# First cross-attention: second scores on 99 rows of the query parts, no rows cleared, first query tile split on VectorE

## The reference, cut to what matters

```python
x = _layernorm(x + _L0_xattn_ref(x, ctx_512, ctx_512), axis=-1)

def _L0_xattn_ref(q, k, v):              # q (4, 512, 512); k = v = ctx_512 (4, 512, 128)
    H, KV, D, G = 32, 8, 16, 4           # 32 query heads on 8 key heads, 16 wide
    qh = q.reshape(B, S, KV, G, D).transpose(0, 2, 3, 1, 4)
    kh = k.reshape(B, S, KV, D).transpose(0, 2, 1, 3)
    vh = v.reshape(B, S, KV, D).transpose(0, 2, 1, 3)
    scores = jnp.einsum('bkgsd,bktd->bkgst', qh, kh) / 4
    weights = jax.nn.softmax(scores, axis=-1)
    out = jnp.einsum('bkgst,bktd->bkgsd', weights, vh)
    return out.transpose(0, 3, 1, 2, 4).reshape(B, S, E)
```

## Time and profile before

| | us |
|---|---|
| median of 3 runs | 5124.7 |
| lowest, highest | 5121.35, 5125.94 |
| the profiled execution's own time | 5129.01 |
| its span, first to last instruction | 5127.8 |
| busy: PE, PEld, DVE, ACT, POOL | 4467.1, 2365.1, 2998.9, 1684.2, 1697.6 |
| mean granted clock of TensorE | 0.931 |

### The profile page before, as it was taken

One profiled execution on the slowest core, in us unless ns is written; L12 is line 12 of the kernel. 1 busy time (PEld: TensorE's weight loads), 2 busy tenths in 40 slices (PEclk: granted clock), 3 DMA queues, 4 the chain that ended last, 5 costly groups with the idle time before them and its releaser, 6 DMA issues.

```text
span 5127.8 us, 65483 instructions
## 1 busy us (share of the span) xinstructions
PE 4467.1 (87%) x22744; PEld 2365.1 (46%) x22744; DVE 2998.9 (58%) x5723; ACT 1684.2 (33%) x3306; POOL 1697.6 (33%) x1861
## 2 busy tenths in 40 slices
PE   7996888899999758887999888849999999798688
PEld 6773222244445543554333333325555555343466
DVE  5885777678876986884555565642332333456622
ACT  1112676622113324664222222212112111355432
POOL 1224222000115863552011112455555554211511
PEclk9997999999998678999999999879999999899899
DMA  4330000010000002000012010118999996400000
GB/s 139 98 93 15 2 2 2 35 55 1 0 0 1 1 10 113 2 1 29 25 29 61 25 45 27 26 29 209 245 233 238 217 224 129 143 1 17 3 15 19
DMA packets 154390, 327.66 MB, mean 64 GB/s; under 512 B 25841, under 2 KB 39665, under 8 KB 152498
## 3 DMA queue, kind: packets, MB, share of 16 engines
q1 hardware_dynamic: 106370, 222.50, 13.4%
q0 software_dynamic: 46976, 100.56, 10.1%
q10 hardware_dynamic: 720, 0.40, 0.0%
HBM read 377.91 MB, written 79.30 MB: 89 GB/s over the span
## 4 chain that ended last, share of the span: by engine, by line
PE 64%; DVE 17%; ACT 6%; POOL 5%; issue 4%; DMA 3%; SPq 0%; DVEq 0%; ACTq 0%; POOLq 0%
PE ps L205 59%; PE ps L210 4%; DVE arena L867 2%; ACT arena L2406 2%; ACT arena L841 1%; DVE ps L1386 1%; DVE ps L1409 1%; DMA moe_y<-arena 1%; DVE arena L2432 1%; POOL moe_slots L2133 1%; DVE arena L248 1%; ACT arena L834 1%; ACT arena L1771 1%; DVE arena L1378 1%; DVE arena L2448 1%
## 5 line engine op out<-in xcount | busy, mean ns | idle before, releaser
L205 PE MATMUL ps<-arena 128*128 128x512 f32 (+14 forms) x18488 | 3918.9, 455 | 369.3 <-ACT arena L1786 50.6
L205 PEld LDWEIGHTS ps<-arena 128*128 128x128 f32 (+3 forms) x18488 | 1842.2, 165 | 2250.2 <-issue 1199.9
L210 PE MATMUL ps<-arena 128*128 128x128 f32 (+2 forms) x3232 | 421.1, 270 | 253.3 <-DVE arena L266 54.7
L210 PEld LDWEIGHTS ps<-arena 128*128 128x128 f32 (+2 forms) x3232 | 344.0, 140 | 425.0 <-issue 200.4
L2891 POOL DMA_INDIRECT moe_y<-arena x191 | 304.9, 1596 | 303.6 <-DVE arena L2860 236.4
L256 POOL TENSOR_SCALAR arena<-arena 128x1 f32<-128x1 f32 x160 | 52.7, 330 | 925.1 <-DVE arena L250 922.4
L2406 ACT ACTIVATE arena<-ps 128x1024 f32<-128x1024 f32 (+3 forms) x256 | 166.2, 701 | 576.2 <-PE ps L205 576.2
L867 DVE TENSOR_REDUCE arena<-ps 128x2 f32<-128x1024 f32 x256 | 303.8, 1218 | 85.9 <-PE ps L205 85.1
L2432 DVE TENSOR_REDUCE arena<-ps 128x2 f32<-128x256 f32 (+3 forms) x256 | 198.8, 819 | 260.4 <-PE ps L205 260.4
L2843 DVE SCALAR_TENSOR_TENSOR arena<-ps,arena 128x128 f32<-128x128 f32 x382 | 103.5, 312 | 411.8 <-ACT arena L2830 409.9
L841 ACT ACTIVATE arena<-ps 128x512 f32<-128x512 f32 x512 | 277.6, 597 | 129.2 <-PE ps L205 126.6
(11 more groups left out here) (312 smaller groups left out, 3939.8 us busy)
## 6 DMA issues: line engine op xcount, KB each, us to landing
arena<-in_L_ffn_gu SPq DMA_DIRECT2D x191, 768.0 KB
arena<-in_L_ffn_dn SPq DMA_DIRECT2D x191, 256.0 KB
arena<-in_L_ffn_dn SPq DMA_DIRECT2D x191, 128.0 KB
arena<-in_L_ffn_w SPq DMA_DIRECT2D x64, 256.0 KB
moe_y<-arena SPq DMA_DIRECT2D x34, 256.0 KB
arena<-in_L_ffn_w_gate SPq DMA_DIRECT2D x32, 256.0 KB
arena<-in_L_ffn_w_up SPq DMA_DIRECT2D x32, 256.0 KB
arena<-in_L_ffn_w_down SPq DMA_DIRECT2D x32, 256.0 KB
```

The source lines that it names most:

```text
L205: return self.nc.tensor.matmul(out, lhsT, rhs, start=start, stop=stop, skip_group_check=True)
L210: return self.nc.tensor.transpose(out, in_, ident[0:n, 0:n])
```

## The change

The second scores contract over 99 rows of `KS` and `QS`. Rows 99 to 127 are read by nothing any more, so `QS` is not cleared, and all of columns 96 to 127 of `kst` are set to ones by one memset, which now stands ahead of the two for `VA`. SyncE's wait for the clears is gone. The nine instructions of the query split become the function `qsplit`, issued on VectorE for tile 0 and on GpSimd for tiles 1 to 15. In `order()`, the split of tile 0 stands ahead of the key tiles. The query transposes of tile 0 wait for VectorE, those of the others for GpSimd, as before.

```diff
--- before.py
+++ after.py
@@ -712,10 +712,10 @@
     qv = qst.rearrange("p h (r d) -> p h r d", d=16)
 
     def order():
+        yield "qsplit", 0, 0
         for t4 in range(4):
             yield "prep", 0, t4
             yield "prep2", 0, t4
-        yield "qsplit", 0, 0
         yield "qt", 0, 0
         yield "qt", 0, 1
         for n in range(16 * NT + LAG + 11):
@@ -755,11 +755,31 @@
     def loads():
         for b in range(4):
             dma.start(sp, CX[:, 4 * b:4 * b + 4, :], ins["ctx_512"][b].rearrange("(t p) d -> p t d", p=P), "ctx", b)
-        sp.wait_ge(pool, "qs0")
         for i in range(NT):
             sp.wait_ge(dve, "mr", i)
             sp.wait_ge(pe, "pv", i - 3, 7) if i >= 3 else None
             dma.start(sp, QS[i % 3][96:99, :, :], MT[i % 2][0:96, :], "mrow", i)
+
+    def qsplit(unit, by, i):
+
+        part = [qv[:, :, r, :] for r in range(6)]
+        sc, res = (a.rearrange("p (h d) -> p h d", d=16) for a in (qsc, qres))
+        by.wait_ge(pool if i > 1 else dve, "qparts", i - 1)
+        unit.tensor_scalar(qsc, k.X[:, i, :], 0.25, 1.0, ALU.mult, ALU.mult).then_inc(*by.done("qsc", i))
+        by.wait_ge(by, "qsc", i)
+        by.wait_ge(pe, "qt", i - 1, 3) if i else None
+        unit.tensor_copy(part[0], sc).then_inc(*by.done("qhi", i))
+        by.wait_ge(by, "qhi", i)
+        unit.tensor_tensor(res, sc, part[0], ALU.subtract).then_inc(*by.done("qr1", i))
+        unit.tensor_copy(part[1], part[0]).then_inc(*by.done())
+        unit.tensor_copy(part[4], part[0]).then_inc(*by.done())
+        by.wait_ge(by, "qr1", i)
+        unit.tensor_copy(part[2], res).then_inc(*by.done("qmid", i))
+        by.wait_ge(by, "qmid", i)
+        unit.tensor_tensor(res, res, part[2], ALU.subtract).then_inc(*by.done("qr2", i))
+        unit.tensor_copy(part[3], part[2]).then_inc(*by.done())
+        by.wait_ge(by, "qr2", i)
+        unit.tensor_copy(part[5], res).then_inc(*by.done("qparts", i))
 
     def tensor():
         for what, i, j in order():
@@ -772,7 +792,7 @@
                 t.then_inc(*pe.done("kt", i, j))
             elif what == "qt":
                 s1 = S1.take("qt", i, j, by=((act, "q", i, 2 * j + 1),))
-                pe.wait_ge(pool, "qparts", i)
+                pe.wait_ge(pool if i else dve, "qparts", i)
                 for u in range(2):
                     bb = s1[:, u, :].bitcast(BF16).rearrange("p (h n) -> p h n", n=P)
                     for h in range(8):
@@ -794,7 +814,7 @@
                 v, t4 = tile(j)
                 bb = S2.take("s2", i, j, by=((act, "p", i, j),))
                 pe.wait_ge(dma, "mrow", i)
-                k.mm(bb, KS[b % 2][:, v, t4 * P:t4 * P + P], QS[i % 3][:, 4 * v:4 * v + 4, :].rearrange("p h n -> p (h n)"), True,
+                k.mm(bb, KS[b % 2][0:99, v, t4 * P:t4 * P + P], QS[i % 3][0:99, 4 * v:4 * v + 4, :].rearrange("p h n -> p (h n)"), True,
                      True).then_inc(*pe.done("s2", i, j))
             elif what == "pv":
                 j, t4 = divmod(j, 4)
@@ -850,7 +870,9 @@
     def vector():
         former = -1, 0
         for what, i, j in order():
-            if what == "prep":
+            if what == "qsplit" and i == 0:
+                qsplit(nc.vector, dve, 0)
+            elif what == "prep":
                 dve.wait_ge(dma, "ctx", i)
                 dve.wait_ge(pool, "kst0")
                 if former[0] >= 0:
@@ -891,15 +913,9 @@
                 k.norm(i)
 
     def gpsimd():
+        nc.gpsimd.memset(kst[:, :, 96:128], 1.0).then_inc(*pool.done("kst0"))
         for buf in VA:
             nc.gpsimd.memset(buf[:, :, :, 16:32], 1.0).then_inc(*pool.done("ones"))
-        nc.gpsimd.memset(kst[:, :, 96:128], 0.0).then_inc(*pool.done("kst00"))
-        pool.wait_ge(pool, "kst00")
-        nc.gpsimd.memset(kst[:, :, 96:99], 1.0).then_inc(*pool.done("kst0"))
-        pool.wait_ge(pool, "kst0")
-        for buf in QS:
-            nc.gpsimd.memset(buf[96:128, :, :], 0.0).then_inc(*pool.done("qs0"))
-        pool.wait_ge(pool, "qs0")
         for what, i, j in order():
             if what == "prep":
                 pool.wait_ge(dma, "ctx", i)
@@ -910,25 +926,8 @@
                 pool.wait_ge(dve, "kparts", i, j)
                 for dst, src in ((2, 0), (3, 1), (5, 0)):
                     nc.gpsimd.tensor_copy(kv[:, :, dst, :], kv[:, :, src, :]).then_inc(*pool.done("kparts", i, j))
-            elif what == "qsplit":
-                part = [qv[:, :, r, :] for r in range(6)]
-                sc, res = (a.rearrange("p (h d) -> p h d", d=16) for a in (qsc, qres))
-                pool.wait_ge(pool, "qparts", i - 1)
-                nc.gpsimd.tensor_scalar(qsc, k.X[:, i, :], 0.25, 1.0, ALU.mult, ALU.mult).then_inc(*pool.done("qsc", i))
-                pool.wait_ge(pool, "qsc", i)
-                pool.wait_ge(pe, "qt", i - 1, 3) if i else None
-                nc.gpsimd.tensor_copy(part[0], sc).then_inc(*pool.done("qhi", i))
-                pool.wait_ge(pool, "qhi", i)
-                nc.gpsimd.tensor_tensor(res, sc, part[0], ALU.subtract).then_inc(*pool.done("qr1", i))
-                nc.gpsimd.tensor_copy(part[1], part[0]).then_inc(*pool.done())
-                nc.gpsimd.tensor_copy(part[4], part[0]).then_inc(*pool.done())
-                pool.wait_ge(pool, "qr1", i)
-                nc.gpsimd.tensor_copy(part[2], res).then_inc(*pool.done("qmid", i))
-                pool.wait_ge(pool, "qmid", i)
-                nc.gpsimd.tensor_tensor(res, res, part[2], ALU.subtract).then_inc(*pool.done("qr2", i))
-                nc.gpsimd.tensor_copy(part[3], part[2]).then_inc(*pool.done())
-                pool.wait_ge(pool, "qr2", i)
-                nc.gpsimd.tensor_copy(part[5], res).then_inc(*pool.done("qparts", i))
+            elif what == "qsplit" and i:
+                qsplit(nc.gpsimd, pool, i)
             elif what == "over":
                 k.norm_rstd(i)
```

## The result

| | before | after |
|---|---|---|
| median of 14 runs each, us | 5125.9 | 5110.5 |
| lowest, highest | 5117.6, 5133.6 | 5102.9, 5115.8 |
| span of the profiled execution | 5127.8 | 5108.9 |
| mean granted clock in it | 0.931 | 0.935 |

The ratio of the runs is 0.9972 with a 95% interval of 0.9964 to 0.9980: 14.4 us faster, between 10.3 and 18.5. The interval of one set is thus 8 to 9 us wide, and the size of the gain is better read from the stage's own length in the trace.

What follows compares the result with a forecast made beforehand. The prediction took the first cross-attention's opening, a chain of single steps, as the bound. Key preparation's 5.5 us plus 5.6 to the first scores made 11.1, taking the median from 5124.7 to 5113.6; range 5108 to 5119.5.

Steps and rivals of the forecast that it cites:

- one of its own signs: First score matmul of the first cross-attention: forecast near 451; wrong if after 453.5 or before 449.5.
- The other two signs: Wrong if the loop to the next stage changes by over 3 us, or 99-row operations differ by over 10 ns.
- The bound: First cross-attention's opening: a chain of single steps, 35.1 us in which TensorE does only 64 small transposes.
- The clears hold VectorE: Stage opening: three GpSimd clears, 10.57 us, hold VectorE's key casts (3.17 for two instead of 0.23 each) and delay GpSimd's copies.
- The split's length: First query split on VectorE, nine instructions: 4.66 us plus 0.8 waiting for memsets, ending at 432.4.
- The first rival: Query split or port lock dearer, split ending up to 434.9: gain 8.6 to 10.2, time 5114.5 to 5116.1; chance 0.22.
- The key preparation: First key split 1.41 us, 0.88 to transposes at 434.7 instead of 440.17; fourth key tile 10.22 later.
- From the last key tile: Fourth key tile at 444.95, then ScalarE's copies are late; first scores at 450.95 instead of 462.04.
- 99 rows: 512 second-score matmuls in the loop: zero cost taken; rival 0.05 us each, 25.6 us, time 5139.2, chance 0.03.
- The clock: TensorE's clock after the first scores: rival has it rise earlier, 4 us more, gain 15, time 5109.6; chance 0.12.
- Within or beyond 0.2%: Whole kernel, resolution 10.25 us (5114.4): faster beyond it 0.62, within it 0.31, slower 0.07.
- the later clock: TensorE's clock rises later or dips once more in the loop: 4 us lost, gain 7, time 5117.7; chance 0.09.

Runs made afterwards that it cites:

- the second: The changed kernel measured again with no edit: ratio 0.9981 to the kernel before, 9.7 us faster, stage of 573.3 us.
- e2: Changed kernel, clears out and 99 rows, but first query split left on GpSimd behind the key tiles: ratio 0.9989 to before, first scores at 27.8 us.
- e3: Changed kernel with GpSimd's clears and 128 rows kept, first query split on VectorE: ratio 0.9991 to before, first scores at 31.9 us.
- e7: Changed kernel with GpSimd's two VA memsets moved behind the key preparation: one run, query split 3.69 us, first scores at 22.16 us.
- e1_rows99: Kernel before with only the second scores cut to 99 rows, clears and GpSimd split kept: ratio 1.0005 to before, loop 551.4 us.

## Why the prediction was right

The forecast was 11.1 us and 5113.6; the opening lost 12.96 and the median of the first set was 5110.5. The mechanism was right and one term was too large. How near the totals lie is partly luck. The stage lost 11.4 us in the first profile, since the opening's 13.0 were met by a loop 1.6 longer with its dips of the clock, and 13.1 in the second. The profiled execution was to take 5117.9 us and took 5110.1: of the 7.8 between, 7.5 lie outside the stage.

By one of its own signs the prediction was off: the first score matmul was not to start before 449.5. It started at 447.51, and counted from the release of the kernel before (426.80 + 22.28) at 449.08, so the opening was better than the forecast allowed for. The forecast had 450.95 there; 1.6 of the 1.9 us between come from the length of the split. The other two signs stayed quiet: the loop changed by 1.6 us and the 99-row matmuls by nothing. Step by step:

- *The bound.* The opening was the chain that the prediction named, and both halves of it are real: the clears (e2, 7.4 us) and the late split (e3, 3.4 with the clears in its way).
- *The clears hold VectorE.* Right, and shown by e3 with casts of 3.81 us that are otherwise 0.41.
- *The split's length.* The one term that was mis-sized. 5.5 us were forecast, 3.9 measured. The three bfloat16 copies take 0.28 in e7, not 0.43 (0.45 us in all). Eight gaps of 0.04 were added, 0.3; measured, a start lies up to 0.08 before the end of the operation ahead (426.86 behind 426.25 + 0.69), and over the nine these overlaps outweigh the gaps by 0.3, so this is another 0.6. The port costs 0.2 to 0.3 rather than 0.8: VectorE's scaling came first, so that GpSimd's first memset did the waiting, and much of the two longer memsets (425.88 to 427.14) lay beside the subtraction (426.25 to 426.94). The whole 1.3 us that the prediction held against its own 0.8 was thus not paid either. With the lower bound of the prediction, 4.06 us without port, the sum would have been right within 0.4 us. The first rival's nine instructions of 0.68 were wrong: casts take 0.41 to 0.51 and copies 0.27 to 0.42.
- *The key preparation.* 1.41, 0.88 and 10.22 us were carried over; measured are 1.3, 1.0 and 10.20.
- *From the last key tile.* 6.0 us forecast; 5.86 measured (441.65 to 447.51), with ScalarE late, as it said.
- *99 rows.* Zero forecast, 382 ns on 99 rows as on 96 and 128, and zero in the loop. The weight loads of 99 rows take 99 ns in their mean, so the one-row load's dearer price did not carry over.
- *The clock.* It did move, but not by the 4 us of the rival. The stretches of 10 us from the first scores on show for before

```profile
482.00:492.00 10.00, 5.12 (x27) 2.18 (x26) 7.53 (x12) 3.21 (x3) 5.97 (x9) 0.67 0.01 2
492.00:502.00 10.00, 9.82 (x39) 2.56 (x40) 7.05 (x6) 5.42 (x10) 0.00 (x0) 0.76 0.00 0
502.00:512.00 10.00, 9.18 (x69) 3.62 (x67) 7.16 (x6) 7.79 (x14) 0.00 (x0) 1.00 0.01 2
```

  and for after

```profile
447.50:457.50 10.00, 8.66 (x18) 1.32 (x18) 8.94 (x8) 0.00 (x0) 5.11 (x8) 0.50 0.01 2
457.50:467.50 10.00, 8.83 (x34) 2.97 (x33) 8.24 (x8) 1.93 (x2) 0.00 (x0) 0.50 0.00 0
467.50:477.50 10.00, 4.75 (x27) 1.90 (x26) 7.90 (x12) 3.21 (x3) 5.96 (x9) 0.84 0.01 3
477.50:487.50 10.00, 9.86 (x42) 2.68 (x40) 7.43 (x7) 5.69 (x11) 0.00 (x0) 0.80 0.00 0
487.50:497.50 10.00, 9.18 (x68) 3.61 (x66) 6.67 (x6) 8.06 (x14) 0.00 (x0) 1.00 0.01 2
```

  (clock in the third column from the end). The first two stretches are at 0.50 in both kernels; the third and fourth have 0.84 and 0.80 after against 0.67 and 0.76 before. TensorE was thus longer at the full clock, and ScalarE's fourth pair of exponentials starts 36.4 us behind the first scores instead of 36.9: 0.5 us. Nor can it be put down to the change: e1_rows99, with the opening of before, has 0.75 and 0.74 in these two stretches, and e2_noclear 0.67 and 0.52, with the fourth pair at 39.5 us and the longest loop, 553.1. Half a microsecond gained there and 1.6 lost over the whole loop are within what the profiles of one kernel differ by (552.7 and 551.0 for the changed kernel).
- *Within or beyond 0.2%.* The first set's interval begins at 10.3 us, just beyond the 10.25; the second's reaches down to 5.1. That the gain lies beyond 0.2% is what the first set says narrowly and the stage's loss in the two profiles (11.4 and 13.1 us) supports.
- *The range.* With the later clock and the dearer split together, its own terms leave 11.1 - 2.5 - 4 = 4.6 us, which is 5120.1 and not 5119.5; nothing hangs on it.

## What to carry to other kernels

At the start of a stage, look for the chain of single steps before the main loop; a fill on GpSimd there costs twice, by its own length and by holding VectorE's casts and copies of data that have nothing to do with it. Ask first whether the filled rows need to be read at all. Then spread the steps over the engines that idle, count buffers (one more for the key parts was worth 4.6 us of 22) and put a step that is ready early ahead of the ones that wait.

## What the runs showed of the hardware

- Which engine waits at the shared port is decided by who comes first, be it by less than 0.1 us: GpSimd's memset of 0.31 us (e2) took 0.60 when VectorE's scaling had begun 0.07 us before it (after), and VectorE's cast of 0.41 took 3.81 when a clear had begun 0.01 us before it (e3).
- A bfloat16 matmul of 512 columns takes 382 ns on 96, 99 and 128 rows alike at a granted clock of 1.00.
- A copy of 512 bfloat16 values in runs of 16, 96 apart, takes VectorE 0.28 us, a cast of 512 float32 values into the same runs 0.41.
- Runs of one kernel scatter by up to 20 us (before, 5113.8 to 5134.0 in 30 runs; the changed kernel, 5103.7 to 5121.6 in 11), along with the mean granted clock (0.935 to 0.930, and 0.936 to 0.930); this is more than the gain that was measured here.
